# The rarely used passes of a graph and expert kernel, moved behind the end of three engines' programs

## What is computed

```python
edge_index = jnp.stack([src, dst])                 # 50000 edges, sorted by dst, 3125 nodes
x = x + _L0_gnn_ref(_layernorm(x), W1, b1, W2, b2, edge_index, 16)
x = x + _L0_ffn_ref(_layernorm(x)[None], gamma, beta, Wr, br, W1, b1, W2, b2)[0]

def _L0_gnn_ref(x, W1, b1, W2, b2, nn_index, k):
    feat = jnp.concatenate([x[tgt], x[src] - x[tgt]], axis=-1)
    h = jax.nn.relu(feat @ W1 + b1)
    msg = h @ W2 + b2
    out = segment_sum(msg, tgt);  deg = segment_sum(ones, tgt)
    return out / (deg + 1e-08)

def _L0_ffn_ref(...):      # layer norm, router, best 2 of 8 experts, gelu between two products
```

## Time and profile before

| | us |
|---|---|
| median of 3 runs | 968.83 (964.46 to 969.68) |
| the profiled execution, device time | 967.21 |
| its span in the trace | 965.5 |
| busy: PE / DVE / ACT / POOL | 856.4 / 652.1 / 617.0 / 620.4 |
| end of the first block, release of its barrier | 78.7 |
| edge pass, until the release of its barrier | 625.0 |
| node stage, until the release of its barrier | 742.1 |

### The profile page before, as it was taken

One profiled execution on the slowest core, in us unless ns is written; L12 is line 12 of the kernel. 1 busy time (PEld: TensorE's weight loads), 2 busy tenths in 40 slices (PEclk: granted clock), 3 DMA queues, 4 the chain that ended last, 5 costly groups with the idle time before them and its releaser, 6 DMA issues. The chain is left out here.

```text
span 965.5 us, 17806 instructions
## 1 busy us (share of the span) xinstructions
PE 856.4 (89%) x4148; PEld 664.7 (69%) x4149; DVE 652.1 (68%) x1665; ACT 617.0 (64%) x1374; POOL 620.4 (64%) x623
## 2 busy tenths in 40 slices
PE   6986999999998899899999898799916999999997
PEld 2434776666666676567766665489815899999996
DVE  5755888888888888778888887566685233333342
ACT  3613888888898888788889898644414434343442
POOL 1035777777777777777777777298005477776774
PEclk9997999999999999989999999899958999999999
DMA  8335787787787788877887788257710244444443
GB/s 261 123 131 173 238 241 236 239 237 246 241 243 238 233 248 239 239 232 238 241 244 239 235 241 255 85 176 224 228 57 17 56 67 78 75 71 75 67 73 43
DMA packets 88145, 171.88 MB, mean 178 GB/s; under 512 B 13735, under 2 KB 53553, under 8 KB 87985
## 3 DMA queue, kind: packets, MB, share of 16 engines
q0 software_dynamic: 44288, 124.29, 46.8%
q1 hardware_dynamic: 42513, 44.74, 15.4%
q10 hardware_dynamic: 1216, 1.44, 0.5%
HBM read 149.44 MB, written 21.37 MB: 177 GB/s over the span
## 5 line engine op out<-in xcount | busy, mean ns | idle before, releaser
L928 POOL DMA_INDIRECT gath<-q_rows,idx_t x416 | 402.6, 968 | 139.0 <-issue 92.7
L972 DVE SCALAR_TENSOR_TENSOR h_lo<-bank,h_hi 128x512 fp32r<-128x512 f32 x334 | 224.6, 683 | 44.8 <-ACT h_hi L1097 42.5
L1097 ACT ACTIVATE h_hi<-bank 128x512 fp32r<-128x512 f32 x334 | 195.4, 597 | 36.6 <-DVE bank L967 14.6
L1085 ACT ACTIVATE bank<-gath 128x512 f32<-128x512 f32 x293 | 176.8, 603 | 29.9 <-DMA gath<-q_rows,idx_t 27.6
L1247 PE MATMUL agg_ps<-h_hi,oh 128*128 128x512 f32 x416 | 165.2, 397 | 0.3 <-DVE h_lo L972 0.3
L1227 PE MATMUL bank<-p_hi,ohT 128*128 x293 | 127.8, 436 | 42.4 <-ACT bank L1085 39.0
L1248 PE MATMUL agg_ps<-h_lo,oh 128*128 128x512 f32 x416 | 164.8, 396 | 0.0
L1808 POOL DMA_INDIRECT out<-y_out,sca_i x56 | 93.1, 1662 | 53.0 <-DMA out<-y_out,sca_i 20.2
L1227 PEld LDWEIGHTS bank<-p_hi,ohT 128*128 128x128 f32 x293 | 55.4, 189 | 96.8 <-issue 89.0
L1860 ACT ACTIVATE actT<-bank,b1T 128x128 f32<-128x128 f32 x224 | 64.3, 369 | 82.0 <-PE bank L1893 81.9
L1228 PE MATMUL bank<-p_lo,ohT 128*128 x293 | 116.6, 398 | 0.0
(11 more groups left out here) (270 smaller groups left out, 1274.0 us busy)
## 6 DMA issues: line engine op xcount, KB each, us to landing
rows_sb<-rel_blocks SPq DMA_DIRECT2D x104, 128.0 KB, 4.3
fw<-in_L_ffn_W SPq DMA_DIRECT2D x16, 512.0 KB, 4.7
gath<-q_rows,idx_t POOLq DMA_INDIRECT x416, 4.3
q_rows<-q_buf SPq DMA_DIRECT2D x25, 256.0 KB, 2.1
out<-x_all SPq DMA_DIRECT2D x28, 128.0 KB, 3.1
x_all<-in_x SPq DMA_DIRECT2D x25, 128.0 KB, 2.5
xm_rows<-xt SPq DMA_DIRECT2D x25, 128.0 KB, 2.3
x_all<-in_x SPq DMA_DIRECT2D x2, 640.0 KB, 12.0
```

The source lines that it names most:

```text
L928: pool.indirect_dma_start(out=gath[:, j % RING, :], out_offset=None, in_=q_rows[:, :], in_offset=bass.IndirectOffsetOnAxis(ap=idx_t[:, j:j ...
L972: dve.scalar_tensor_tensor(out=h_lo[:, j % LO_RING, :], in0=z_of(slot0, j), scalar=0.0, in1=h_hi[:, j % HI_RING, :].bitcast(F32), op0=ALU. ...
L1085: actv.activation(z_of(slot0, j), gath[:, j % RING, :], ACT.Copy).then_inc(s_seed, 1)
L1097: actv.activation(h_hi[:, j % HI_RING, :], z_of(slot0, j), ACT.Relu).then_inc(s_hi, 1)
```

## The change

The value `n_pass` is loaded on DVE, ACT and PE ahead of the first pass and kept in a register. After the first pass stands only a comparison with 2. The loop over further passes is written out after the experts' block's instructions of the same engine, with a jump around it there, and with a jump back to the point behind the comparison. POOL's own loop stays where it was.

```diff
+        def branch_to_further(eng, one_pass):
+            name = eng.engine.name
+            further[name], branched[name] = one_pass, nc.cur_bb
+            eng.br_lt(passes[name], 2, on_true=f"past_{name}", on_false=f"further_{name}")
+            nc.switch_bb(f"past_{name}")
+
+        def further_passes(eng):
+            name = eng.engine.name
+            eng.br(f"over_{name}")
+            with nc.body(f"further_{name}", parent=branched[name], valid_engines=[eng.engine]):
+                with eng.Fori(1, passes[name]) as p:
+                    further[name](p)
+                eng.br(f"past_{name}")
+            nc.switch_bb(f"over_{name}")
...
+                passes[actv.engine.name] = actv.value_load(n_pass[0:1, 0:1], min_val=1, max_val=NT)
                 one_pass(0)
-                n = actv.value_load(n_pass[0:1, 0:1], min_val=1, max_val=NT)
-                with actv.If(n > 1):
-                    with actv.Fori(1, n) as p:
-                        one_pass(p)
+                branch_to_further(actv, one_pass)
...                       (the same for dve and pe)
@@ the experts' block, at the end of the lists of DVE, ACT and PE @@
+                further_passes(actv)
```

More of the change, by code:

```diff
@@ L833, in build @@
         assert NS % UNROLL == 0 and SC * P > NS and UNROLL % RING == 0 and RING % Z_RING == 0
+        passes, further, branched = {}, {}, {}
+        def branch_to_further(eng, one_pass):
[11 more added lines that the diff above has]
+            nc.switch_bb(f"over_{name}")
         def first_pass(eng, prologue, step, per_trip=None):
@@ L1052, in one_pass @@
                         trips(dve, p, prologue, one, per_trip)
+                passes[dve.engine.name] = dve.value_load(n_pass[0:1, 0:1], min_val=1, max_val=NT)
                 one_pass(0)
@@ L1061, in _ @@
                                   down_nt[0:NG, :].unsqueeze(1).to_broadcast([NG, GROUP, NT + 1]), ALU.is_equal).then_inc(s_gcol, 1)
-                n = dve.value_load(n_pass[0:1, 0:1], min_val=1, max_val=NT)
-                with dve.If(n > 1):
-                    with dve.Fori(1, n) as p:
-                        one_pass(p)
+                branch_to_further(dve, one_pass)
             @block.scalar
@@ L1337, in one_pass @@
                         trips(pe, p, prologue, one, per_trip)
+                passes[pe.engine.name] = pe.value_load(n_pass[0:1, 0:1], min_val=1, max_val=NT)
                 one_pass(0)
@@ L1345, in _ @@
                 ins.then_inc(s_deg, 1)
[L1346 to L1349, removed]
+                branch_to_further(pe, one_pass)
         s_fw = sem("s_fw")
@@ L1843, in _ @@
                     dve.tensor_scalar(y_out[:, i % OUTS, :], y_out[:, i % OUTS, :], w_slot[:, i:i + 1], None, ALU.mult).then_inc(s_y, 1)
+                further_passes(dve)
             @block.scalar
@@ L1918, in _ @@
                     second_product(i)
+                further_passes(pe)
 _INS = ["x", "src", "dst", "L0_gnn_W1", "L0_gnn_b1", "L0_gnn_W2", "L0_gnn_b2", "L0_ffn_gamma", "L0_ffn_beta",
```

## The result

| | before | after |
|---|---|---|
| median of 19 runs, us | 967.14 (964.46 to 969.68) | 964.25 (961.95 to 966.82) |
| ratio after / before, 95% interval | | 0.9966 (0.9956 to 0.9976) |
| profiled execution: span, us | 965.5 | 960.3 |
| first block's release | 78.7 | 78.1 |
| edge pass: from there to ACT's count of `s_closed` | 542.6 | 542.4 |

The changed kernel is 0.34% faster, with an interval of 0.24% to 0.44%. The rows that answer to the earlier trace rows: the barrier behind the edge pass stands at L892 now, ACT's count at L1195, the comparison at L841 for all three engines.

A forecast was written before the change was run, and what follows sets the result against it. The prediction took ACT's load and long jump ahead of the barrier after the edge pass as the cost: 968.83 - 3.3 = 965.5 us, set to 965.2 because the median leans high, nothing charged elsewhere; range 961.8 to 968.6.

The forecast's parts named there:

- ACT is the last, 3.5 us of nothing, 2.75 of it the jump: Barrier after the edge pass: ACT arrives last after 3.5 us without computation, 2.75 of it the long jump over further passes.
- What the next engine allows: Same barrier: without load and jump ACT stays last, PE some 0.3 us ahead, so the release comes 3.3 us earlier.
- the open price of 1.68: Barrier after the edge pass: PE's drain might last 1.68 us, as at the final barrier, cutting the gain to 2.2.
- Only the load goes: Rival at the barrier after the edge pass: ACT's 2.75 us stay, gain only 0.6 us, 968.2 us; 8 in 100.
- PE keeps its 3.46 us: Rival at the barrier after the edge pass: PE's long comparison stays, gain 1.1 us, 967.7 us; 9 in 100.
- The front: Program start: the loads moved there are hidden by other waits, nothing charged; without cover 0.5 us.
- The end: Final barrier: long jumps of some 3 us stay hidden, DVE 1.5 us ahead of POOL; uncovered, they cost from 4.5 us on.
- The clock: Node stage start: a shorter pause might keep PE's clock up, giving 1.5 us; uncharged; as rival, 4.8 us gain, 10 in 100.
- Slower by code that comes late elsewhere: Rival, node stage and experts' block: late instruction blocks cost about 3.3 us each, two giving 972.1 us; 7 in 100.

The follow-up runs named there:

- the masked pair: Kernel before and changed kernel, each with one more register step (a mask) at semaphore waits whose value comes from memory; first timing 967.11 and 964.42 us.
- the 14 jumps: Changed kernel with masks plus 14 jumps over 32 to 512 never-run instructions on DVE, ACT and PE after the experts' block; no total time given.
- the masked one: Changed kernel with a mask step at semaphore waits whose value comes from memory; 964.42 us, ratio 0.9981 to the kernel before; timed again, 965.88 us.
- the jump away only: Changed kernel with masks, but each load of n_pass back behind the first pass; 964.83 us, ratio 0.9981 to the kernel before.
- the late patterns: Changed kernel with masks, POOL's five node-stage index patterns moved behind its bias loop; 962.95 us, ratio 0.9965 to the kernel before; timed again, 964.82 us.

## Why the prediction was right

Forecast were 965.2 us, a gain of 3.3 (0.34%), and the way there; measured are 964.25 and 0.34% (the two medians are 2.9 us apart). Against 967.14, the median of all runs of before, the forecast gain gives 963.8. That the full seam shows in the time rests on this one pair; the masked pair gave 2.0 us of 3.3.

- *ACT is the last, 3.5 us of nothing, 2.75 of it the jump.* Right. Without jump and load ACT's drain follows its count by 0.16 us (0.2 forecast), and the seam fell by 3.4. The halves run by themselves give 2.9 for the jump and 0.4 to 0.8 for the load, forecast 2.75 and 0.6.
- *What the next engine allows.* Right: PE was ready 0.2 us ahead of ACT (0.3 forecast). Its drain ended with the last degree product, 0.918 us after it began; the open price of 1.68 did not come.
- *Only the load goes*, and *PE keeps its 3.46 us.* Both out. PE's comparison takes 0.096 us when it falls through, and an unconditional jump on PE takes 3.6. By the rule that I drew from the Trainium skill (Advanced Engine Details and Errata, ISA Cache), with a 128 KB store on TensorE, a jump over 384 instructions should have found its target; it took 3.74 us here. What PE has at hand reaches further than on the others (256 cost 0.4 us, while 192 cost 2.7 to 2.9 on DVE and ACT), but not as far as that. The record was long because PE waited for code all the same, as its transfers on q8 show.
- *The front.* Nearly right. ACT's load took 0.487 us there and not 0.284, and the first seed comes 5.5 us after the release instead of 5.1. DVE's first `oh` comes 0.9 us later too, but its first `ohT` still waits 1.47 us for a transfer. No cost of it shows in the pass, 542.4 us against 542.6; but the pass takes 541.2 to 544.5 us in the profiles of this study, so 0.4 us could not be told there.
- *The end.* Right: jumps of 2.5 to 3.6 us, DVE 2 us ahead of POOL (1.5 forecast). In other profiles PE's takes up to 4.4 us there, beside POOL's transfers.
- *The clock.* No gain at the first tiles, as forecast, by POOL's 2.97 us. The first 3 us of the stage run at the lower clock as before, in spite of a pause of 0.6 us only. The prediction set the low clock beside 4.1 us of idling. But the clock stood at 0.50 from 621.4 on already before the change, 0.3 us after the last degree product, and with the change from 620.5 on, 0.2 us after it; so the long pause was not needed for the fall, and the 1.5 us that a shorter one might have given back were not to be had. Here from the view of busy time by stretch (PE, PEld, DVE, ACT, POOL, then the clock):

```profile
620.50:620.90 0.40, 0.00 (x0) 0.00 (x0) 0.00 (x0) 0.00 (x0) 0.00 (x0) 0.50 0.00 0
...
621.00:624.00 3.00, 3.00 (x11) 2.58 (x12) 1.89 (x4) 1.20 (x2) 2.12 (x6) 0.51 0.00 0
624.00:627.00 3.00, 3.00 (x17) 2.64 (x17) 0.97 (x3) 0.60 (x1) 2.90 (x5) 1.00 0.01 3
```

- *Slower by code that comes late elsewhere.* Not seen: PE is busy 59.0 of 59 us from 631 to 690, and the experts' block takes 223.3 us in both.

The two spans differ by 5.2 us, 1.7 more than the seam. 0.6 lie in the first block, which the change doesn't touch, 0.2 in the pass, and 0.9 in the node stage, late in it: the clock falls 71.5 us after the release before, 74.8 after it in the profile of the change.

The same view of both, before first, each over the 3.3 us that begin there or at the like place:

```profile
696.50:699.80 3.30, 2.80 (x14) 2.70 (x14) 1.02 (x13) 1.75 (x3) 0.00 (x0) 0.50 1.01 343
```

```profile
692.30:695.60 3.30, 1.69 (x14) 1.51 (x13) 1.82 (x16) 1.67 (x2) 0.00 (x0) 1.00 0.98 321
```

At 0.50 the 14 products keep PE busy for 2.80 us, at 1.00 for 1.69. The short stage is not the change's: the two profiles in which the clock falls late have it (74.8 and 116.1 us in the profile of the change, 74.9 and 116.2 with the 14 jumps), while other kernels with the same change, as the masked one (72.0 and 117.0) and the one with the jump away only (71.5 and 117.0), do not. The place of the fall is not all there is to it: the second profile of the masked change has 73.5 and 117.5. The gain of 0.34% in the time needs no more than the seam.

## What to carry to other kernels

Code that normally doesn't run costs some tenths of a us while it is passed over by a short jump, and some 3 us on each engine once the jump leads beyond what the engine has at hand. Where several engines meet at a barrier behind such code, it has to go from all of them: here ACT alone gave nothing, ACT and PE half. Its place is where the jump over it waits beside something longer, and the records of the sequencers, not those of the computation, show the price, and the list of transfer queues shows the code being brought in.

## What the runs showed of the hardware that I had not expected

- The reach differs by engine: on DVE and ACT jumps over 128 instructions cost 0.45 to 0.55 us and over 192 cost 2.7 to 2.9; on PE 256 cost 0.42 and 384 cost 3.74. Transfers of instructions have 16,384 bytes on the queue that goes with PE's jumps (q8) and 8,192 on the other (q14).
- A long jump on PE has three parts: 0.95 to 1.7 us until the transfer starts, 0.88 to 1.5 for it, 1.3 to 1.6 until PE goes on (fifteen jumps).
- The pause stands in different places of the trace: on PE inside the comparison's record (3.3 to 4.4 us), on ACT and DVE behind a record of 0.04 to 0.08 us.
- DVE's addition on 128x25 values takes 1.26 us while POOL writes its index patterns (1.255 to 1.258 in twelve profiles) and 0.18 us without them (two profiles of the kernel with the late patterns). The patterns take 1.5 us in all.
